# Attention inside a transformer block: unrolled, with three score banks in a ring and the token-row transposes in the banks of the maxima

## The reference

```python
xn = _layernorm(x, axis=-1)
# attention: 16 heads of 16 numbers
Q = (xn @ Wq.T).reshape(16, 4, 1024, 16)      # K and V alike
scores = jnp.einsum('hbqd,hbkd->hbqk', Q, K)
out = jnp.einsum('hbqk,hbkd->hbqd', softmax(scores), V).reshape(4, 1024, 256)
y = out + xn
attention = (y - mean(y, (1, 2))) / sqrt(var(y, (1, 2)) + 1e-5)
# experts: 8, the best 2 per token
gates = softmax over the two largest of xn @ w_gate.T, 0 elsewhere
experts = sum over e of gates[:, e] * ((xn @ w_in[e].T) @ w_out[e].T)
result = x + attention + experts
```

## Time and profile before

| | |
|---|---|
| runs: median (lowest to highest) | 1115.41 us (1113.98 to 1117.44) |
| the profiled execution's own span | 1116.5 us |
| 64 blocks of the attention, start of block 0 to the last value matmul | 331.7 to 1103.5 us |
| TensorE / VectorE / ScalarE / GpSimd busy | 1077.7 / 850.5 / 654.6 / 172.1 us |

### The profile page before, as it was taken

One profiled execution on the slowest core, in us unless ns is written; L12 is line 12 of the kernel. 1 busy time (PEld: TensorE's weight loads), 2 busy tenths in 40 slices (PEclk: granted clock), 3 DMA queues, 4 the chain that ended last, 5 costly groups with the idle time before them and its releaser, 6 DMA issues.

```text
span 1116.5 us, 25452 instructions
## 1 busy us (share of the span) xinstructions
PE 1077.7 (97%) x7752; PEld 550.3 (49%) x7752; DVE 850.5 (76%) x1171; ACT 654.6 (59%) x1256; POOL 172.1 (15%) x364
## 2 busy tenths in 40 slices
PE   7999999999999999999999999999999999999995
PEld 6888878887663333333333333333333333333332
DVE  6333377777897888888878888888888888888876
ACT  3333311211216777777777777777777777777775
POOL 2221033533320011001001101001100101100100
PEclk9999999999998999999999999999999999999998
DMA  8999699888520111111111111111111111111104
GB/s 268 386 325 334 223 169 201 164 201 172 150 67 25 47 37 37 47 37 37 46 37 35 45 40 35 42 43 34 40 45 35 40 46 34 37 47 35 38 20 151
DMA packets 127227, 107.48 MB, mean 96 GB/s; under 512 B 58848, under 2 KB 96480, under 8 KB 127200
## 3 DMA queue, kind: packets, MB, share of 16 engines
q1 hardware_dynamic: 73696, 64.93, 20.5%
q10 hardware_dynamic: 53504, 42.21, 13.9%
HBM read 68.56 MB, written 38.54 MB: 96 GB/s over the span
## 4 chain that ended last, share of the span: by engine, by line
PE 50%; SPq 18%; DMA 14%; issue 4%; DVE 1%; ACT 1%; POOL 0%; POOLq 0%; ACTq 0%; DVEq 0%
PE ps L981 15%; PE ps L1013 13%; SPq L328 11%; PE ps L1003 11%; PE ps L1025 10%; DMA max_d<-mt 8%; DMA qf<-max_d 5%; SPq L341 4%; SPq L332 3%; PE ps L1034 2%; DMA xttl<-xtl_d 1%; ACT wp L600 0%; DVE stage L900 0%; SPq L360 0%; DVE negm L775 0%
## 5 line engine op out<-in xcount | busy, mean ns | idle before, releaser
L775 DVE TENSOR_REDUCE negm<-ps 128x1 f32<-128x1024 f32 x512 | 603.5, 1219 | 124.6 <-PE ps L1003 123.7
L600 ACT ACTIVATE wp<-ps 128x512 f32<-128x512 f32 x1024 | 555.9, 595 | 223.1 <-PE ps L1013 222.8
L1013 PE MATMUL ps<-qf,kf 99*128 99x512 bf16 x1024 | 324.3, 386 | 16.6 <-DMA qf<-max_d 14.3
L1025 PE MATMUL ps<-wp,vb 128*17 128x256 f32 x4096 | 272.7, 383 | 0.0
L1003 PE MATMUL ps<-kf,qf 96*128 96x512 bf16 x1024 | 265.9, 380 | 1.5 <-DVE negm L775 1.5
L1013 PEld LDWEIGHTS ps<-qf,kf 99*128 99x128 bf16 x1024 | 81.6, 97 | 243.5 <-issue 108.6
L1003 PEld LDWEIGHTS ps<-kf,qf 96*128 96x128 bf16 x1024 | 98.2, 97 | 125.2 <-issue 5.8
L1025 PEld LDWEIGHTS ps<-wp,vb 128*17 128x17 f32 x4096 | 94.0, 97 | 109.6 <-issue 60.8
L981 PE MATMUL ps<-mth,xtth 128*128 128x512 f32 x256 | 104.8, 409 | 3.0 <-DMA xttl<-xtl_d 1.9
L981 PE MATMUL ps<-mtl,xtth 128*128 128x512 f32 x256 | 102.0, 399 | 0.0
L981 PE MATMUL ps<-mth,xttl 128*128 128x512 f32 x256 | 101.9, 398 | 0.0
(11 more groups left out here) (107 smaller groups left out, 644.9 us busy)
## 6 DMA issues: line engine op xcount, KB each, us to landing
wp<-w_in SPq DMA_DIRECT2D x16, 512.0 KB, 4.7
wp<-w_out_t SPq DMA_DIRECT2D x16, 512.0 KB, 6.0
qk_d<-stage ACTq DMA_DIRECT2D x8, 1024.0 KB, 4.7
third_d<-wp ACTq DMA_DIRECT2D x32, 256.0 KB, 2.6
qf<-third_d SPq DMA_DIRECT2D x64, 96.0 KB
kf<-third_d SPq DMA_DIRECT2D x64, 96.0 KB
v_d<-vstage ACTq DMA_DIRECT2D x8, 544.0 KB, 3.7
vb<-v_d SPq DMA_DIRECT2D x128, 34.0 KB, 2.7
```

The source lines that it names most:

```text
L600: nc.scalar.activation(wp[:, kt % 4, h * HALF:(h + 1) * HALF], ps[:, ST_BANK[h], :], ACT.Exp).then_inc(exp_done[h], 1)
L775: nc.vector.tensor_reduce(negm[:, par, qt:qt + 1], ps[:, b:b + 2, :].rearrange("p b c -> p (b c)"), AX.X, ALU.max, negate=True).then_inc(m ...
L1013: nc.tensor.matmul(ps[:, ST_BANK[h], :], kf[0:SR, u, kt * P:(kt + 1) * P], qf[0:SR, u, h * HALF:(h + 1) * HALF], start=True, stop=True).th ...
L1025: last = nc.tensor.matmul(ps[32 * j:32 * j + VW, PV_BANK, 0:POS // 4], vb[:, par, kt, :], wp[:, kt % 4, j * (POS // 4):(j + 1) * (POS // 4 ...
```

## The change

On all five engines the loops over blocks become straight-line code with constant semaphore values, all 64 blocks. The arithmetic and the number of matmuls, exponentials, reductions and transfers stay, bf16 scores included. Apart from that:

- The scores get a third bank, 7, and the banks 4, 5, 7 are used in turn as a ring. A unit of scores is now one half h of the queries with two key tiles, j and j + 4, two matmuls; one semaphore counts all exponentials, and one wait, for the first exponential of the unit before, stands ahead of both matmuls of a unit.
- TensorE's order for each j = 0 to 3 is: unit h = 0, one `max_scores`, unit h = 1, one `max_scores`, then `sum_values` of the two key tiles of j - 1.
- The token-row transposes lose their bank. They take a turn of the two pairs of maximum banks, behind the fifth maximum of an even block; maxima and token rows share one count of turns, and each turn waits for the one two before it to be read.
- On ScalarE the copy of the sums stands behind the four exponentials of j = 0. The exponentials ask for the scores first and then, at h = 0, for the place in `wp`; before, it was the other way round.
- On VectorE the reciprocals and the product stand together behind the fifth maximum of an even block, the statistics behind the second of an odd one.
- SyncE's order is the same. Ahead of the first block TensorE waits for all four expert banks (before: two) and for the memset of bank 6.
- At the end the two small means use the banks 1 and 3.

```diff
-        ST_BANK = (4, 5)
+        ST_BANK = (4, 5, 7)
...
+        for n in range(2):
+            for qt in range(NKT):
+                max_turn[n, qt] = next_turn()
+        for n in range(NB):
+            for qt in range(NKT):
+                if n + 2 < NB:
+                    max_turn[n + 2, qt] = next_turn()
+                if qt == 4 and n % 2 == 0 and n > 0:
+                    row_turn[n // 2 - 1] = next_turn()
+        row_turn[NB // 2 - 1] = next_turn()
+
...
-            def step(i, u):
-                n = SLOTS * i + u
-
-                sp.wait_ge(pv_done[3], 2 * n)
-                values(n + 1, (u + 1) % 2)
-                m = u + 1
-                max_rows(m % SLOTS, m % 2, n + 1, 3 * (i if u == 0 else i + (m - 2) // SLOTS + 1),
-                         2 * i + m // 2)
-
-            def step_features(i, u):
-
-                for h in range(2):
-                    sp.wait_ge(st_ready[h], NKT * (SLOTS * i + u + 1))
-                features(SLOTS * i + u + SLOTS, u)
-
-            with sp.Fori(0, NB // SLOTS - 1) as i:
-                for u in range(SLOTS):
-                    step(i, u)
-                    step_features(i, u)
-            for u in range(SLOTS - 1):
-                step(NB // SLOTS - 1, u)
-
+            for n in range(NB - 1):
+                if n:
+                    sp.wait_ge(pv_done, NKT * n)
+                values(n + 1)
+                max_rows(n + 1)
+                if n + SLOTS < NB:
+                    for half in range(2):
+                        sp.wait_ge(st_ready[half], NKT * (n + 1))
+                    features(n + SLOTS)
...
-            def exps(n, kt):
-                for h in range(2):
-                    act.wait_ge(pv_done[kt % 4], 2 * n + kt // 4)
-                    act.wait_ge(st_ready[h], NKT * n + kt + 1)
-                    nc.scalar.activation(wp[:, kt % 4, h * HALF:(h + 1) * HALF], ps[:, ST_BANK[h], :],
-                                         ACT.Exp).then_inc(exp_done[h], 1)
-
-            def pv_out_at(i, u):
-                n = SLOTS * i + u
-                act.wait_ge(pv_done[3], 2 * n + 2)
-                act.wait_ge(tr_done, 2 * i + u // 2)
-                nc.scalar.copy(ot[:, :, u % 2, :], ps[:, PV_BANK, 0:4 * TB].rearrange("p (g t) -> p g t", t=TB)
+            def exps(n, j, h):
+                unit = NKT * n + 2 * j + h
+                for b in range(2):
+                    act.wait_ge(st_ready[b], unit + 1)
+                    used = NKT * n + 2 * j + b - 4
+                    if h == 0 and used >= 0:
+                        act.wait_ge(pv_done, used + 1)
+                    nc.scalar.activation(wp[:, j % 2 * 2 + b, h * HALF:(h + 1) * HALF], ps[:, ST_BANK[(2 * unit + b) % 3], :],
+                                         ACT.Exp).then_inc(exp_done, 1)
+
+            def pv_out(n):
+                act.wait_ge(pv_done, NKT * (n + 1))
+                if n >= 2:
+                    act.wait_ge(turn_ready, row_turn[n // 2 - 1] + 1)
+                nc.scalar.copy(ot[:, :, n % 2, :], ps[:, PV_BANK, 0:4 * TB].rearrange("p (g t) -> p g t", t=TB)
                                ).then_inc(pv_evac, 1)
 
-            def step(i, u, before=True):
-                for kt in range(NKT):
-                    exps(SLOTS * i + u, kt)
-                    if kt == 2 and before:
-
-                        pv_out_at(i if u else i - 1, (u - 1) % SLOTS)
-
-            for u in range(SLOTS):
-                step(0, u, before=u > 0)
-            with act.Fori(1, NB // SLOTS) as i:
-                for u in range(SLOTS):
-                    step(i, u)
-            pv_out_at(NB // SLOTS - 1, SLOTS - 1)
-
+            for n in range(NB):
+                for j in range(NKT // 2):
+                    exps(n, j, 0)
+                    exps(n, j, 1)
+                    if j == 0 and n:
+                        pv_out(n - 1)
+            pv_out(NB - 1)
 
...
+            for n in range(NB - 2):
+                for qt in range(NKT):
+                    maxima(n + 2, qt)
+                    if qt == 1:
+                        max_transpose(n + 1)
+                    if n % 2 == 0 and n and qt == 4:
+                        normalise(n // 2 - 1)
+                    if n % 2 == 1 and n > 1 and qt == 1:
+                        statistics((n - 1) // 2 - 1)
...
-            def max_scores(i, u, n, qt):
-
+            def free_turn(turn):
+                if turn >= 2:
+                    pe.wait_ge(turn_done, turn - 1)
+
+            def max_scores(n, qt):
+                u, turn = n % SLOTS, max_turn[n, qt]
                 if qt == 0:
-                    pe.wait_ge(feat_in[u], 96 * (i + 1))
-                pe.wait_ge(max_done[qt % 2], 4 * n + qt // 2)
-                for h in range(2):
-                    last = nc.tensor.matmul(ps[:, MAX_BANK[qt % 2] + h, :], qf[0:FR, u, qt * P:(qt + 1) * P],
-                                            kf[0:FR, u, h * HALF:(h + 1) * HALF], start=True, stop=True)
-                last.then_inc(max_ready[qt % 2], 1)
-
-            def scores(i, u, n, kt):
-
-                if kt == 0:
-                    pe.wait_ge(mrow_in[u], 48 * (i + 1))
-                for h in range(2):
-                    pe.wait_ge(exp_done[h], NKT * n + kt)
-                    nc.tensor.matmul(ps[:, ST_BANK[h], :], kf[0:SR, u, kt * P:(kt + 1) * P],
+                    pe.wait_ge(feat_in[u], 96 * (n // SLOTS + 1))
+                free_turn(turn)
+                for half in range(2):
+                    last = nc.tensor.matmul(ps[:, MAX_BANK[turn % 2] + half, :], qf[0:FR, u, qt * P:(qt + 1) * P],
+                                            kf[0:FR, u, half * HALF:(half + 1) * HALF], start=True, stop=True)
+                last.then_inc(turn_ready, 1)
+
+            def scores(n, j, h):
+                u, unit = n % SLOTS, NKT * n + 2 * j + h
+                if j == 0 and h == 0:
+                    pe.wait_ge(mrow_in[u], 48 * (n // SLOTS + 1))
+                if unit:
+                    pe.wait_ge(exp_done, 2 * unit - 1)
+                for half in range(2):
+                    tile = j + half * NKT // 2
+                    nc.tensor.matmul(ps[:, ST_BANK[(2 * unit + half) % 3], :], kf[0:SR, u, tile * P:(tile + 1) * P],
                                      qf[0:SR, u, h * HALF:(h + 1) * HALF], start=True, stop=True
-                                     ).then_inc(st_ready[h], 1)
-
-            def sum_values(n, par, gen, kt):
-
-                if kt == 0:
-                    pe.wait_ge(vb_in[par], 32 * (gen + 1))
-                    pe.wait_ge(pv_evac, n)
-                for h in range(2):
-                    pe.wait_ge(exp_done[h], NKT * n + kt + 1)
-                for j in range(4):
-                    last = nc.tensor.matmul(ps[32 * j:32 * j + VW, PV_BANK, 0:POS // 4], vb[:, par, kt, :],
-                                            wp[:, kt % 4, j * (POS // 4):(j + 1) * (POS // 4)],
-                                            start=kt == 0, stop=kt == NKT - 1, tile_position=(0, 32 * j))
-                last.then_inc(pv_done[kt % 4], 1)
+                                     ).then_inc(st_ready[half], 1)
+
+            def sum_values(n, j, b):
+                if j == 0 and b == 0:
+                    pe.wait_ge(vb_in[n % 2], 32 * (n // 2 + 1))
+                    if n:
+                        pe.wait_ge(pv_evac, n)
+                pe.wait_ge(exp_done, 2 * (NKT * n + 2 * j + 1) + b + 1)
+                for c in range(4):
+                    last = nc.tensor.matmul(ps[32 * c:32 * c + VW, PV_BANK, 0:POS // 4], vb[:, n % 2, j + b * NKT // 2, :],
+                                            wp[:, j % 2 * 2 + b, c * (POS // 4):(c + 1) * (POS // 4)],
+                                            start=j == 0 and b == 0, stop=j == NKT // 2 - 1 and b == 1,
+                                            tile_position=(0, 32 * c))
+                last.then_inc(pv_done, 1)
 
             def to_token_rows(pair):
+                turn = row_turn[pair]
                 pe.wait_ge(pv_evac, 2 * pair + 2)
-                pe.wait_ge(norm_done, pair)
+                free_turn(turn)
                 for g in range(4):
-                    last = nc.tensor.transpose(ps[:, TR_BANK, g * P:(g + 1) * P],
+                    last = nc.tensor.transpose(ps[:, MAX_BANK[turn % 2], g * P:(g + 1) * P],
                                                ot[:, g].rearrange("p b t -> p (b t)"), ident[:])
-                last.then_inc(tr_done, 1)
+                last.then_inc(turn_ready, 1)
...
-            for j in range(2):
+            for j in range(E // 2):
                 pe.wait_ge(ff_added[j], 2 * NT)
...
+            pe.wait_ge(att_const, 3)
...
+            for n in range(NB):
+                for j in range(NKT // 2):
+                    for h in range(2):
+                        scores(n, j, h)
+                        if n + 2 < NB:
+                            max_scores(n + 2, 2 * j + h)
```

(60 more changed lines are left out.)

139 lines of the change are left out of this document (49 added, 90 removed).

## The result

The changed kernel takes **1145.78 us** (median of four runs, 1144.79 to 1147.43) against 1114.70 (1113.18 to 1117.44) for the kernel before in the same comparison: a ratio of 1.0288, 95% interval 1.0259 to 1.0317. It is slower by 31.1 us; the forecast was +35.6.

The account below looks back on a forecast made before the run. TensorE, 97% busy, was taken as the bound, SyncE's chain next. Per pair of blocks +1.17 us, times 29 = 34, plus 1 for blocks 2 and 3 and 1 for late rows: 1151 us against 1115.41; range 1135 to 1169.

Parts of the forecast that it names:

- The second unit: TensorE, each j: second score pair waits for an exponential, starting 1.08 us after the first; j 3.05 us, 0.167 more.
- Token rows: Third j of even blocks: sixth maximum waits for the fifth's reduction; j 3.88 us, 0.83 over the others, before 0.49.
- The tail: Blocks 62 and 63, without maxima: 2.61 us per j, 22.5 us to the end as today; taken as 0.
- The pair of blocks: Blocks 4 to 62, per two blocks: all terms together +1.17 us, times 29 = 34 us.
- the copy on ScalarE: Copy of the sums behind the exponentials of j = 0 delays the next exponential: 0.03 us per block.
- late rows of maxima: SyncE's chain when maxima take 4.0 us to land instead of 2.9: 1 us for all such cases.
- The wait for the row of the maxima: TensorE ahead of even blocks: SyncE's chain no longer holds it up, so 0.57 us per pair goes.
- unrolling: Loops written out on every engine: no gap of instruction supply expected, taken as 0.
- The beginning: Block 0: waits some 1.5 us later, but second unit meets the same reduction and slow clock: 0, give or take 1.5.
- The ring: Rival, faster: three score banks free TensorE, second unit under 0.9 us after the first; 1101 us; 8%.
- The cancelling of gains and losses: Rival, no change: shorter delay, j at 2.90, and transposes that hide; 1114 us; 4%.
- The clock: Rival: TensorE's short idles lower its granted clock, a 6 us half-speed stretch in each pair; 1240 us; 3%.

Follow-up runs that it names:

- e2: Changed kernel, common wait kept, but both maximum tiles of a j between its two score units as before the change: 1124.92 us, ratio to before 1.0091.
- e1: Changed kernel, but each score matmul waits only for the exponential that read its own bank: 1102.47 us, ratio to before 0.9889.
- e4: Changed kernel, but exponentials ask first for their place in wp, then for the scores, as before: 1160.60 us, ratio to before 1.0400.
- e6: Kernel before, only TensorE's order changed: one maximum tile behind each key tile; two banks, loops and waits kept: 1203.12 us, ratio 1.0827.
- e3: Changed kernel, token-row transposes taking the turn behind the sixth maximum and standing behind that j's value matmuls: 1134.67 us, ratio to before 1.0170.
- e8: Kernel before with attention loops written out, and exponentials asking for the scores first, then their place: 1102.45 us, ratio 0.9912.
- e7: Kernel before with only its attention loops written out as straight-line code on all five engines: 1115.20 us, ratio 1.0025.
- e5: Changed kernel with the edits of e1 and e3, and SyncE issuing the next values while the maxima are landing: 1083.12 us, ratio to before 0.9740.

## Why the prediction was right, point by point

**The second unit, +0.167 per j.** Right in kind and size: predicted 1.08 us and 3.05, measured 1.08 and 3.04, which is +0.163. The step that decided, that 0.87 us of work lie between a score matmul and a wait that takes 1.08, is borne out from both sides: more work between (e2) or the right bank's wait (e1) takes the loss away, a slower round trip (e4) raises it by its own amount, and the order alone makes it in the kernel before (e6).

**Token rows, 3.88 us.** Measured 3.88, with the reduction as releaser, and 11 us back where they are moved (e3). **The tail** of 2.61 us per j:

```profile
1108.39 0.61 PE L949 MATMUL ps<-qf,kf 99*128 99x512 bf16 x2
...
1110.99 0.61 PE L949 MATMUL ps<-qf,kf 99*128 99x512 bf16 x2
```

2.60 us; from block 62 to the end of the span it is 34.6 us, 35.0 before.

**The pair of blocks, +1.17.** Block 4 starts at 378.98 us and block 62 at 1108.39: 29 pairs of 25.15 us, +1.094 against 24.06. Of the 0.08 that I had too much, 0.06 is the copy on ScalarE: at 445.45 to 445.82 us it doesn't delay the exponential at 445.74, which starts 0.42 us after its scores (445.32) as any other. The term was 0. So was the 1 us for late rows of maxima.

**The wait for the row of the maxima, -0.57 per pair.** It went, as said, but there is a second reason that I had left out: I costed unrolling at nothing on all engines. On TensorE that holds (2.88 us in e8); on SyncE it takes 1.04 us off the chain in e8, and less in the changed kernel. There the longer blocks would have covered the chain anyway (11.45 against 12.15), so the sum didn't suffer; my expectations of e1 and e2 did.

**The beginning, 0 give or take 1.5.** In the two profiled executions this term was mis-sized. Block 4 starts at 378.98 us instead of 383.82, 4.84 early, though blocks 1 to 3 are 0.87 longer: the beginning gained 5.7. 1.33 of it lie ahead of block 0, which starts at 330.34 instead of 331.67. These say little about the change: e7 and e8, with the same code up to there, start block 0 at 329.29 and 334.16. In block 0 itself, 11.34 us against 15.72, lie 4.38. I had said that its second unit would wait for the same reduction and then for the same slow clock. TensorE in the kernel before:

```profile
334.21 0.61 PE L1003 MATMUL ps<-kf,qf 96*128 96x512 bf16 x2 [1.51 <-DVE negm L775]
```

and in the changed kernel:

```profile
330.34 0.59 PE L949 MATMUL ps<-qf,kf 99*128 99x512 bf16 x2 [1.50 <-DVE ps L759]
...
331.49 0.61 PE L949 MATMUL ps<-qf,kf 99*128 99x512 bf16 x2
```

With one maximum tile at a time the reductions keep pace, TensorE goes on, and the granted clock stays at 1.00 from 336 to 342 us where it was 0.50. That this is due to the order isn't shown: the slow stretch is absent in the profiles of e1, e2, e3, e5 and e6, present in those of e7 and e8, and also in that of e4, which has the order of the changed kernel (here its row; in e7 and e8 the clock of that stretch is 0.60 and 0.67):

```profile
336.00:342.00 6.00, 6.00 (x29) 1.81 (x28) 2.89 (x4) 2.68 (x6) 0.00 (x0) 0.57 0.03 5
```

The executions of one kernel differ in this too: in the seven of e8 the mean granted clock of the whole span goes from 0.991 (1107.26 us) to 0.996 (1099.45 us). What decides it stays open.

**The sum.** 29 x 1.094 = 31.7, less 4.84 and 0.4, is 26.5 us, the difference of the two spans (1143.0 and 1116.5). A run's time is 1.8 us over its span, so the profiled execution of before was 3.6 us over the median of its four runs, and that of after 1.0 under: 26.5 + 4.6 = 31.1. Against the medians the beginning may thus have been right after all: 31.7 for the pairs, 0.9 for blocks 1 to 3 and -0.4 for the tail make 32.2, which leaves -1.1 of the 31.1 for block 0 and all ahead of it. This is an estimate, as it takes the rest to be alike in all executions. The 4.5 us by which the forecast was too high are then the copy (1.7), the beginning (1.1), the late rows (1) and smaller sizes elsewhere.

**The rivals.** The ring did not free TensorE as the change has it: its condition, a second unit within 0.9 us, was missed by 0.18. e1, which meets it, came out at the rival's time (1102.5 against 1101), in part by luck: the rival had the token rows at 0.83 us and a wait for the row of the maxima, where e1 shows 1.06 (3.89 less 2.83) and next to none. Nor is e1's gain over the kernel before the ring's alone, since e8 takes 1102.45 us with two banks.

The Trainium skill, Perfetto Trace Analysis, section Matmuls, says that independent groups should rotate through different PSUM banks, so that evacuation overlaps the next group. The j of 2.83 us in e1, e2 and e5 against 2.88 in e8 agrees with it. The changed kernel rotates too and is slower than two banks, since its wait is for an evacuation that hasn't had time to end.

The cancelling of gains and losses fell with the same wait, 1.08 us where it needed 0.93, and with the transposes, which didn't hide. The clock didn't fall in the attention either: in the profile of after it is 1.00 from 432 to 1081 us, with a second unit that comes some 0.2 us late in each j. The to and fro of the clock that the Trainium skill, TensorE: Matmul & The Clock Gate, section A second HAM failure mode: psum-queue depth-cycling, describes for short pauses between groups isn't seen there.

## What to carry to other kernels

Ahead of a ring of buffers, write down for each wait how long ago the awaited work was begun and how long its round trip takes (here 1.08 us from matmul through exponential to the next matmul); a third buffer was a loss here because two things came together: the order of the work shortened the distance (1.30 to 0.87 us), and one wait for a group asked for the release that only its later member needs. Reckon this by distances of starts on the timeline: the busy share fell by one point, and the chain of waits showed TensorE alone. A gain beside a change can belong to something else in it: here writing the loops out shortened SyncE's chain, and the ring itself was worth 0.05 us per j. A step that takes a turn in another step's ring also takes that step's wait.

## What was not expected of the hardware

In written-out code the order of two waits ahead of one ScalarE instruction is worth 0.06 us: 0.48 us from scores to exponential where the wait that ends last is asked last (e4 and e7), 0.42 where it is asked first (the changed kernel and e8). In the loop of the kernel before it was 0.42 with that wait asked last; why the loop differs wasn't tested. And a DMA issue on SyncE is no dearer in a loop, but the short instructions around each are: 6.24 us (kernel before) against 5.20 (e8) for the same eight issues.
